# Spreading eight embedding gathers over the first eight steps of a batch, in a transformer tower on one core

## What is computed

```python
h = emb_table[x] @ W_e2h + b_e2h                  # gather of 1024 rows of 128 floats per batch
for i in range(6):                                # conv1d over the sequence, 128 -> 256 channels, 3 taps
    a, g = split(conv1d(h, conv_w[i]) + conv_b[i])
    h = (a * sigmoid(g) + h) * 0.7071
h = h @ W_h2e + b_h2e
n = layernorm(h)                                  # then two softmax attentions of 8 heads over 1024 keys
A1, A2 = softmax(q1 k1), softmax(q2 k2)           # mixed by a gate made of window statistics of A1 and A2
h = h + (alpha * A1 + (1 - alpha) * A2) @ v @ Wo
h = h + ffn(layernorm(h))                         # layernorm, linear, expert by token block, linear, gelu
```

## Time and profile before

| | |
|---|---|
| timed runs | 6050.68, 6056.63, 6056.67 us; median 6056.63 us |
| span of the profiled execution | 6159.6 us, from the first to the last instruction; no other time of that execution is given |
| span less median | 103.0 us |
| busy share | PE 86%, DVE 83%, ACT 84%, POOL 40% |
| chain that ended last | PE 54%, issue 14%, DVE 13%, ACT 10%, POOL 5% |

### The profile page before, as it was taken

The page is one execution under the profiler, slowest core; times in us unless marked ns, Lnnn a source line. Parts: engine busy times, 40 slices in busy tenths (PEclk is TensorE's granted clock), DMA queues, the critical chain, the costliest instruction groups (busy, mean ns, idle before and its releaser), DMA issues.

```text
span 6159.6 us, 116651 instructions
## 1 busy us (share of the span) xinstructions
PE 5323.7 (86%) x34070; PEld 2463.4 (40%) x34070; DVE 5116.9 (83%) x5665; ACT 5198.9 (84%) x7937; POOL 2450.5 (40%) x4439
## 2 busy tenths in 40 slices
PE   6988989889898988889889898988889889898985
PEld 4443424334343443434334343443434334343442
DVE  1988889888888988889888888988888888888982
ACT  2988889889898988889889897888888889898884
POOL 6525344352433425344252433425344252433422
PEclk8999999999999999999999999999999999999997
DMA  1001010010101001010010101001010010101000
GB/s 38 19 21 26 18 28 20 21 26 22 26 19 27 20 20 26 19 28 19 21 26 22 26 19 27 20 21 26 22 26 18 22 25 22 26 19 27 20 21 12
DMA packets 164901, 140.60 MB, mean 23 GB/s; under 512 B 89197, under 2 KB 108269, under 8 KB 164141
## 3 DMA queue, kind: packets, MB, share of 16 engines
q1 hardware_dynamic: 159100, 124.09, 8.8%
q0 software_dynamic: 4352, 8.92, 0.7%
q10 hardware_dynamic: 816, 0.02, 0.0%
HBM read 21.26 MB, written 8.91 MB: 5 GB/s over the span
## 4 chain that ended last, share of the span: by engine, by line
PE 54%; issue 14%; DVE 13%; ACT 10%; POOL 5%; SPq 1%; another core or an unknown queue 1%; ACTq 0%; DMA 0%; DVEq 0%; POOLq 0%
PE ps_w L387 21%; PE ps_t L387 11%; PE ps_o L387 11%; PE ps_s L387 10%; DVE rowmin L715 7%; ACT junk L577 4%; DVE negmax L710 4%; ACT exps L583 2%; SPq L328 1%; DVE bn L727 1%; ACT hpre L632 1%; DVE o_raw L723 1%; ACT stage L587 1%; POOL part L855 1%
## 5 line engine op out<-in xcount | busy, mean ns | idle before, releaser
L710 DVE TENSOR_REDUCE negmax<-ps_s 128x1 f32<-128x1024 f32 x2048 | 2491.5, 1217 | 805.8 <-PE ps_s L387 695.9
L577 ACT ACTIVATE junk<-ps_s,negmax 128x1024 bf16<-128x1024 f32 x2048 | 2295.5, 1121 | 288.8 <-DVE rowmin L715 278.3
L715 DVE TENSOR_REDUCE rowmin<-ps_s 128x1 f32<-128x1024 f32 x2048 | 2486.7, 1214 | 0.0
L583 ACT ACTIVATE exps<-ps_t 128x1024 f32<-128x1024 f32 x2060 | 2122.3, 1030 | 314.3 <-PE ps_t L387 173.6
L387 PE MATMUL ps_s<-kst,qst 96*128 96x512 bf16 x4096 | 1293.8, 398 | 520.7 <-ACT junk L577 461.4
L387 PE MATMUL ps_o<-exps,v_cur 128*32 128x256 f32 x16512 | 1381.8, 408 | 159.5 <-DVE o_raw L723 130.0
L387 PE MATMUL ps_t<-qst,kst 99*128 99x512 bf16 x4120 | 1305.8, 400 | 85.8 <-ACT exps L583 70.4
L387 PE MATMUL ps_w<-xc,cw 128*128 128x256 f32 x4704 | 1178.6, 387 | 0.0
L387 PEld LDWEIGHTS ps_w<-xc,cw 128*128 128x128 f32 x4704 | 914.3, 195 | 215.4 <-issue 9.5
L855 POOL TENSOR_SCALAR ctmp<-ug 128x256 f32<-128x256 f32 x408 | 165.8, 406 | 1602.8 <-ACT ug L652 1587.4
L387 PEld LDWEIGHTS ps_s<-kst,qst 96*128 96x128 bf16 x4096 | 343.8, 100 | 1106.8 <-ACT junk L577 828.0
(11 more groups left out here) (179 smaller groups left out, 3902.4 us busy)
## 6 DMA issues: line engine op xcount, KB each, us to landing
qst<-part SPq DMA_DIRECT2D x1542, 32.0 KB, 2.0
kst<-part SPq DMA_DIRECT2D x1542, 32.0 KB, 2.0
qst<-mrow SPq DMA_DIRECT2D x1028, 1.5 KB
out_dram<-z SPq DMA_DIRECT2D x17, 512.0 KB, 3.2
fc1s<-in_fc_w SPq DMA_DIRECT2D x17, 256.0 KB
fc2s<-in_fc_w SPq DMA_DIRECT2D x17, 256.0 KB
cw<-in_conv_w SPq DMA_DIRECT2D x1, 2304.0 KB
odif<-in_table,idx POOLq DMA_INDIRECT x136
```

The source lines that it names most:

```text
L577: nc.scalar.activation(junk[:, n % 2, :], ps_s[:, n % 2, :], ACT.Exp, bias=negmax[:, r, t:t + 1], accum_out=sumsq[:, r, t:t + 1]).then_inc ...
L583: nc.scalar.activation(exps[:, n % RING, :], ps_t[:, :, :].rearrange("p c q -> p (c q)"), ACT.Exp, scale=0.5).then_inc(s_exp, 1)
L710: nc.vector.tensor_reduce(negmax[:, r, t:t + 1], ps_s[:, n % 2, :], axis=AX, op=ALU.max, negate=True)\
L715: nc.vector.tensor_reduce(rowmin[:, r, t:t + 1], ps_s[:, n % 2, :], axis=AX, op=ALU.min)\
```

## The change

Before, one task `gather` in step 0 issues the eight indirect DMAs, one for each block of 128 tokens. Now there are eight tasks, `("gather", t)` in step t. Each stands behind the other tasks of its step but ahead of `msplit`, which `plan` adds last. The waits (indices, PE) stay with gather 0. `embT` may start at step T + 2 = 10 instead of T - 2 = 6, and comes in step 11. The number and size of all operations are as before.

```diff
-PRE = [("gather",)] + two("embT") + two("e2h") + CONV + two("h2e") + [("ln1",)] + two("xnT") + QK[0] + two("v")
+GATHER = [("gather", t) for t in range(T)]
+PRE = GATHER + two("embT") + two("e2h") + CONV + two("h2e") + [("ln1",)] + two("xnT") + QK[0] + two("v")
...
-POOL_COST = {"msplit": 8, "unit": 5, "qk": 35, "convg": 23, "gather": 85, "snap": 80, "alpha": 46, "hcopy": 20,
+POOL_COST = {"msplit": 8, "unit": 5, "qk": 35, "convg": 23, "gather": 11, "snap": 80, "alpha": 46, "hcopy": 20,
...
-    for n, task in {0: ("gather",), 2: ("vcopy", 0), 3: QK[1][0], 5: QK[1][1], 8: QK[1][2], 10: QK[1][3],
+    for n, task in {2: ("vcopy", 0), 3: QK[1][0], 5: QK[1][1], 8: QK[1][2], 10: QK[1][3],
                     14: ("vcopy", 1)}.items():
         at[n].append(task)
-
-    post, pre = [list(POST), T + LAG_V % T + 2], [list(PRE[1:]), T - 2]
+    for t in range(T):
+        at[t].append(GATHER[t])
+
+    post, pre = [list(POST), T + LAG_V % T + 2], [list(PRE[T:]), T + 2]
...
                 if kind == "gather":
                     b = 0 if phase == "pre" else i + 1
-                    pool.wait_ge(s_idx, 16 if phase == "pre" else i * 16 + 32)
-                    w("pe", None)
-                    pool.nop(nofuse=True)
-                    for t in range(T):
-                        nc.gpsimd.indirect_dma_start(out=emb[:, t, :], out_offset=None, in_=table[:, :],
-                                                     in_offset=bass.IndirectOffsetOnAxis(ap=idx[:, t:t + 1], axis=0))\
-                            .then_inc(s_emb, 16)
+                    t = tk[1]
+                    if t == 0:
+                        pool.wait_ge(s_idx, 16 if phase == "pre" else i * 16 + 32)
+                        w("pe", None)
+                        pool.nop(nofuse=True)
+                    nc.gpsimd.indirect_dma_start(out=emb[:, t, :], out_offset=None, in_=table[:, :],
+                                                 in_offset=bass.IndirectOffsetOnAxis(ap=idx[:, t:t + 1], axis=0))\
+                        .then_inc(s_emb, 16)
```

More of the change, by code:

```diff
@@ L989, in task @@
                 last.then_inc(side_sem["pool"], 1)
-            task("pre", 0, PRE[0])
+            for tk in GATHER:
+                task("pre", 0, tk)
             for t in (v_next, v_cur, h_cur):
@@ L1003, in _ @@
             pool.wait_ge(s_init, 4)
-            for tk in PRE[1:]:
+            for tk in PRE[T:]:
                 task("pre", 0, tk)
```

## The result

The changed kernel takes 6109.39 us (median of 4 runs, 6104.24 to 6116.02) against 6056.65 us (4 runs, 6050.68 to 6061.64) on the same chip: a ratio of 1.0089 (95% interval 1.0076 to 1.0101), slower by 53 us. The forecast was 6101 us.

The account below looks back on a forecast made before the run. Every step was taken as bound by DVE or PE. Terms of +2.7 - 2.1 + 1.8 + 0.4 = +2.8 us a batch, x 16 = +45 us, took 6056.6 to 6101 us, range 6045 to 6135.

Parts of the forecast that it names:

- The sign and the mechanism: Slower, chance 0.72: gathers behind POOL's splits delay msplit 1, so DVE, ACT, PE and SP wait at step 8.
- The stall as absent from the timed runs: Steps 2 and 3 lose 7.0 us a batch in the trace, read as a recording cost the timed runs lack.
- The delay: Step 8: msplit 1 ends late behind gathers 3 to 6, mrow 1 waits; +2.7 us a batch, bounds 0 and 2.9.
- Emptying the row: Batch start: only gathers 0 to 2 and vcopy run in a row, some 4.5 us instead of 11; worth 0.
- the spare time: Step 8 before the change: msplit 1 ends 1.26 us ahead of mrow 1, which starts without waiting.
- The clock: After the step 8 wait PE's idle time may lower its clock; +0.4 us a batch, bounds 0 and 2.3.
- The rival that priced it at 2.3 us: Clock falls at step 8 every batch, step 93 costs 1.8 us: 6.2 a batch, 6156 us; 0.2 of slower's 0.72.
- Refilled steps: Convolution halves return in steps 88, 93 and 97, with step 98 also slower; together +1.8 us a batch.
- The last gather: Issued behind msplit around step 9, lands before the first transpose in step 11; worth 0, 2 us to spare.
- Moved side work: Transposes, e2h and convolution halves leave steps 6 to 15: -1.9 us in steps 9 to 15, -0.2 in step 7.
- The stall is real and goes: Rival: the stall of steps 2 and 3 is in timed runs and is removed; 5990 us, chance 0.14.
- The delay is hidden: Rival: the msplit delay costs nothing, leaving -0.3 us a batch; 6052 us, no change, chance 0.14.

Follow-up runs that it names:

- e2_half_ahead: The changed kernel with gathers 5 and 6 moved behind msplit 1 to join gather 7, gathers 3 and 4 staying ahead; 6069.93 us, ratio 1.0023.
- e1_row: The changed kernel with all eight gathers back in a row in step 0, its other plan changes kept; 6032.79 us, ratio 0.9962 to the kernel before.
- e6_row_qk_early: e1_row with the four qk tasks of the first attention one step earlier; 5982.82 us, ratio 0.9877 to the kernel before.
- e10_vcopy_late: e6_row_qk_early with vcopy 0 listed in step 7, behind msplit 1, instead of step 2; 6003.52 us, ratio 0.9913 to the kernel before.

## Why the prediction was right, step by step

**The sign and the mechanism** were right. The gathers that POOL meets between the splits delay `msplit` 1, and DVE, and with it PE and ACT, wait in step 8. Undoing that place alone takes the loss away (0.9962), putting other POOL work there brings it back (1.0116), and the number of gathers between the first split and `msplit` sets the size (5.90, 3.73, 2.38 us).

**The stall as absent from the timed runs** was right, and it decided the sign: 12 us go with the gathers, not 112. The reason given, "a cost of recording the trace", is not supported. The same kernel recorded again has no such stall, nor has any of the ten other profiles here, those with eight gathers in a row among them, and in each of them time and span agree within 3 us. The timed runs too have spans on record, so recording as such does not cost 7 us a batch. It belonged to one execution of before. What "remote" hid can be read from that trace's semaphore events, which the view doesn't name: DVE and ACT waited for PE's own signals. PE's rows before the long step:

```profile
876.69 0.61 PE L387 MATMUL ps_t<-qst,kst 99*128 99x512 bf16 x2 [0.17 <-issue]
877.78 0.61 PE L387 MATMUL ps_s<-kst,qst 96*128 96x512 bf16 x2 [0.49 <-ACT junk L577]
```

The signals for these came at 883.06 and 883.10, 4.7 us or more after the modelled ends; most of the other long waits of this kind in the trace end with a PE signal 4 to 6 us late. What held PE back is not shown, that execution's own time is not known and nothing brought the stall back, so its cause stays open. The Trainium skill's "NOTIFIC — the notification-queue block", section 7.1, was brought in for it; no run here shows that this block held PE. By the Trainium skill's "SBUF — State Buffer", section "Who interferes with whom", gather traffic could not stop PE; the profiles with eight gathers in a row and no stall agree with that; the first trace, with PE held up while gathers ran, is the exception, and its cause is what stays open.

**The terms of the sum**, us a batch, against the table's two kernels in their undisturbed profiles (before traced again, and after):

```
                                     predicted   measured
mrow 1 waits for msplit 1 (step 8)     +2.7        +3.1    5.90 - 2.81
side work out of steps 0 to 7          -0.2        -0.5    19.09 - 19.55
steps 9 to 15, with the clock          -1.5        -0.7    18.10 - 18.80
steps 16 to 87                          0           0.0    209.32 - 209.35
refilled steps, 88 to 127              +1.8        +1.3    112.97 - 111.63
sum                                    +2.8        +3.3    365.38 - 362.13
```

Sixteen times 3.25 is 52 us, and 53 were measured. Single executions vary by more than that match suggests: the second profile of the changed kernel has 365.94 us a batch, 3.8 above the kernel before.

*The delay* of `msplit` 1 came out at nearly the forecast sum, by other parts. Times from the start of step 0, mean of the 15 later batches, us, taken from the start and end of these instructions on POOL and DVE:

```
                          first split  second split  msplit 1  DVE ready for  mrow 1
                          starts       starts        ends      mrow 1         starts
before, first trace         16.66        22.32        27.66       29.00       28.92
before, traced again        11.84        16.40        21.73       21.94       22.18
after                       10.27        17.23        24.75       21.45       24.87
e2_half_ahead               10.35        17.32        22.65       21.53       22.78
```

I had `msplit` 4.0 us later, with 1.26 us to spare. In the undisturbed profiles it ends 3.0 us later: the pairs of gathers cost 2.4 and 2.2 us (I had 1.5, for the gap in the earlier trace rows that isn't there undisturbed, and 2.5), but the first split starts 1.6 us sooner, because the rest of the row no longer stands ahead of it. Emptying the row I had priced at 0, since in the earlier trace rows the stage was what came last. And the spare time is 0.2 us in the mean, not 1.3: in the first trace the stall held DVE back and POOL caught up. The 0.5 us by which DVE comes to `mrow` 1 sooner only lengthens the wait, to 3.4 us. So the term was wrong by about 0.9 us for the first pair and 1.1 for the spare time in one direction, and by 1.6 for the row and 0.3 for the second pair in the other. All but the last come from one source, a trace read beside its stall as if the stall were not there. That they nearly cancelled is luck.

*The clock* was taken at +0.4 as something that may or may not happen. It happens in every batch: in the records the clock falls in step 10 or 11 of all 16 batches, in both profiles of the changed kernel; in the kernel before it falls in steps 6 to 11 of 2 batches. Step 11 takes 3.27 us instead of 2.62, where the prediction had looked for the bare 2.26 in steps 9 to 12. The kernel with two gathers ahead has the same emptied steps without the fall (step 11 at 2.26): its steps 9 to 15 take 17.0 us, 1.8 under the kernel before, close to the 1.9 forecast; `e1_row`, `e6_row_qk_early` and `e10_vcopy_late`, where the clock seldom falls there, take 17.0 to 17.2. In the changed kernel's two profiles they take 18.1 and 17.9. So the clock, as far as this comparison of kernels tells, costs about 1 us a batch and eats half of that gain. The rival that priced it at 2.3 us and added the full cost of step 93 was right on the frequency and priced it too high.

*Refilled steps.* Steps 88, 97 and 98 cost +0.44, +0.57 and +0.44 us (predicted +0.5, +0.5, +0.4). Steps 93 and 94 together went from 7.00 to 6.82 us, 7.15 in the second profile: both ends I had named came true at once, step 93 at +1.18 and step 94 at -1.36, in sum -0.2 or +0.15 where +0.3 was taken. Why the clock falls there was not tested apart.

*The last gather* was right at 0: in neither profile of the changed kernel does PE wait for a gather.

*Moved side work* can be seen alone in the kernel with the gathers in a row: it gains 0.4 us in steps 0 to 7 and 1.6 in 9 to 15, near the 2.1 forecast, and 0.5 in 24 to 87; it pays 0.3 in step 8 and 0.7 in 88 to 127, in sum -1.4 us a batch where -2.1 + 1.8 = -0.3 was forecast. What was off there is the refilled end, 0.7 for 1.8, and the 0.5 us in the middle, which had been put at nothing. Neither is a fixed size: over the six profiles with this end of the plan and `qk` as before, steps 88 to 127 cost 0.7 to 2.0 us more than in the kernel before, most of it by how often step 93 runs long.

**The rivals.** *The stall is real and goes*: fell by the kernels above. *The delay is hidden*: fell by the waits, 75.4 us of them for `mparts` against 25.3. What that rival said of the remainder, 6052 us and no change, was itself wrong: `e1_row` came out 0.4% faster.

## What to carry to other kernels

An engine queue has no step clock: "one per step" put these gathers not in their steps but in a bunch behind whatever POOL starts late, so each item should be priced by what stands behind it there and by who waits for that. Take spare time and gaps only from a profile whose span agrees with the timed runs: behind a stall every engine stands otherwise to its neighbours. Where one hand-over (here `msplit` to `mrow`) is found short of time, look for the others of its kind: moving the four `qk` tasks one step earlier gained 1.0%, more than anything done to the gathers, about half of it at the hand-over and half at the load of unit 0 that starts sooner.

## What the hardware showed that I had not expected

Small shifts in one place seem to change in which steps the granted clock falls elsewhere. With `vcopy` 0 late, step 8 is 0.8 us shorter, and in the clock records of that execution half clock appears in steps 23 (3 batches), 41 (4), 43 or 44 (3) and 51 (5), where the kernel without the edit has none from 23 to 51; steps 24 to 87 take 187.51 against 185.31 us. The kernel with five gathers behind `msplit` shows the same at 23, 41, 44 and 51 (187.42 us). The gain of 13 us that was there to be had became a loss of 21. The mean granted clock of every run goes the same way, 0.962 to 0.964 in the four runs without the edit and 0.955 to 0.959 in the five with it. But the falls vary between executions of one kernel too: in the two profiles of the changed kernel step 23 has half clock in none and in 2 batches, step 51 in 2 and in 4. The profile with `vcopy` 0 late is moreover the slowest of its runs, 34 us above the other in the sum of 16 batches where the medians are 21 apart. That the clock is the cause is read from the records and was not tested apart; why it falls in those steps stays open.

One execution of a kernel whose timed runs agree within 0.3% can carry a stall of 7.0 us in each batch, 112 us in all, that none of the eleven other profiles of this study shows.
